# Moving the sum of the keys' rotary rotation from VectorE to GpSimd, in every step of an attention kernel

## The reference, cut to what matters

```
q = (ln(h) @ w_q)   # 16 heads of 128
k = (ln(h) @ w_k)   # 4 key heads of 128, each shared by 4 query heads
q = q * cos + rotate_half(q) * sin
k = k * cos + rotate_half(k) * sin
scores = q k^T / sqrt(128) + causal mask (window 256)
out = softmax(scores) @ v ; h = h + out @ w_o
```

## Time and profile before

| what | value |
|---|---|
| median of 3 runs | 804.98 us |
| the profiled execution | 805.23 us |
| its span, first to last instruction | 803.3 us |
| mean granted TensorE clock | 0.996 |
| PE busy | 736.1 us (92%) |
| DVE busy | 574.5 us (72%) |
| ACT busy | 445.2 us (55%) |
| POOL busy | 433.7 us (54%) |
| DMA, mean over the span | 39 GB/s |

### The profile page before, as it was taken

How to read it: one execution, slowest core, us unless ns; L and a number is a source line. 1 busy time by engine, 2 the same in 40 slices (tenths; PEclk the granted TensorE clock), 3 DMA queues, 4 the chain that set the end, 5 groups by cost and what they waited for, 6 DMA issues and landing times.

```text
span 803.3 us, 19511 instructions
## 1 busy us (share of the span) xinstructions
PE 736.1 (92%) x6910; PEld 670.9 (84%) x6910; DVE 574.5 (72%) x1602; ACT 445.2 (55%) x1237; POOL 433.7 (54%) x647
## 2 busy tenths in 40 slices
PE   0266788999999999999999999999999999999996
PEld 0156768999999999999989999999999998988883
DVE  6999967887765666766674565665666678888986
ACT  5734445665565657555574555555565656455422
POOL 1397866744434747544474564444384746565622
PEclk9999999999999999999999999999999999999999
DMA  9023751100010203000001020000020000001303
GB/s 209 13 52 77 169 151 34 47 8 8 7 47 8 67 8 96 10 7 7 7 26 41 1 93 8 7 7 3 5 68 7 29 8 8 7 7 25 87 14 91
DMA packets 38127, 31.59 MB, mean 39 GB/s; under 512 B 23790, under 2 KB 29294, under 8 KB 38070
## 3 DMA queue, kind: packets, MB, share of 16 engines
q1 hardware_dynamic: 37926, 30.78, 14.9%
q10 hardware_dynamic: 144, 0.07, 0.0%
HBM read 20.34 MB, written 10.49 MB: 38 GB/s over the span
## 4 chain that ended last, share of the span: by engine, by line
PE 83%; DVE 6%; POOL 4%; ACT 3%; issue 2%; DMA 1%; DVEq 0%; SPq 0%; POOLq 0%
PE bank_quad L1541 17%; PE bank_quad L1542 17%; PE bank_quad L1543 16%; PE bank_pair L1541 4%; PE bank_pair L1542 4%; PE bank_pair L1543 4%; PE bank_quad L1661 2%; PE bank_pair L1732 2%; PE bank_pair L1742 2%; PE bank L1742 2%; PE bank L1746 2%; PE bank L1541 2%; PE bank_quad L1553 2%; PE bank L1542 2%; PE bank L1543 1%
## 5 line engine op out<-in xcount | busy, mean ns | idle before, releaser
L1541 PE MATMUL bank_quad<-xt_hi,w_hi 128*128 128x256 f32 (+1 forms) x568 | 159.5, 281 | 0.0
L1542 PE MATMUL bank_quad<-xt_hi,w_lo 128*128 128x256 f32 (+1 forms) x568 | 158.9, 280 | 0.0
L1543 PE MATMUL bank_quad<-xt_lo,w_hi 128*128 128x256 f32 (+1 forms) x568 | 158.6, 279 | 0.0
L649 POOL TENSOR_TENSOR swap<-swap,cst 128x512 f32<-128x512 f32 (+1 forms) x96 | 105.5, 1110 | 38.4 <-ACT swap L876 38.4
L933 ACT ACTIVATE sm<-sm,mx 128x128 f32<-128x128 f32 (+1 forms) x256 | 113.6, 444 | 20.1 <-DVE mx L1407 20.1
L1238 DVE TENSOR_TENSOR kq<-kq,swap 128x512 f32<-128x512 f32 (+1 forms) x96 | 89.9, 956 | 25.9 <-POOL swap L649 24.8
L1541 PEld LDWEIGHTS bank_quad<-xt_hi,w_hi 128*128 128x128 f32 x568 | 106.8, 188 | 0.0
L1542 PEld LDWEIGHTS bank_quad<-xt_hi,w_lo 128*128 128x128 f32 x568 | 106.7, 188 | 0.0
L1543 PEld LDWEIGHTS bank_quad<-xt_lo,w_hi 128*128 128x128 f32 x568 | 106.3, 187 | 0.0
L689 POOL TENSOR_SCALAR sm<-sm,rinv 128x128 f32<-128x128 f32 (+1 forms) x256 | 103.9, 417 | 0.1
L945 ACT ACTIVATE ot_hi<-bank_quad 128x512 fp32r<-128x512 f32 x64 | 37.8, 597 | 118.4 <-PE bank_quad L1543 118.4
(11 more groups left out here) (343 smaller groups left out, 2132.3 us busy)
## 6 DMA issues: line engine op xcount, KB each, us to landing
mixed<-st SPq DMA_DIRECT2D x32, 128.0 KB
x<-mixed SPq DMA_DIRECT2D x32, 128.0 KB, 3.1
out<-x SPq DMA_DIRECT2D x32, 128.0 KB, 2.3
raw<-in_w_qkv SPq DMA_DIRECT2D x8, 384.0 KB, 3.9
raw<-in_w_o SPq DMA_DIRECT2D x10, 256.0 KB, 2.9
norm_mem<-in_w_qkv SPq DMA_DIRECT2D x6, 384.0 KB, 4.4
later_v<-v_next SPq DMA_DIRECT2D x16, 128.0 KB, 1.7
v_next<-later_v SPq DMA_DIRECT2D x16, 128.0 KB, 2.0
```

What stands on the lines that cost most here:

```text
L649: nc.gpsimd.tensor_tensor(view(sw), view(sw), table(sinT), ALU.mult).then_inc(rot_sin, 1)
L1541: mmul(dst, lh, rh, start=start and k == 0, stop=False, skip_group_check=True)
L1542: mmul(dst, ll, rh, start=False, stop=False, skip_group_check=True)
L1543: last = mmul(dst, lh, rl, start=False, stop=stop and k == n - 1, skip_group_check=True)
```

## The change

The sum of part 0, the keys, leaves DVE. POOL makes it (`keys_add`) straight behind its own product of the keys with the sines, in the prologue and in every step. It waits for `kq_cos` and `rot_sin` and signals a new semaphore, `keys_rot`. ACT waits for that one ahead of rounding the keys and ahead of the next pair's swap; the counts of `kq_rot` are now two in a pair. Three calls of `rope_add(..., 0)` go out of DVE's program.

```diff
+            def keys_add(s):
+                view, _, _, _ = rope_view(0)
+                pool.wait_ge(kq_cos, s * 3 + 1)
+                pool.wait_ge(rot_sin, s * 3 + 1)
+                nc.gpsimd.tensor_tensor(view(kq), view(kq), view(sw), ALU.add).then_inc(keys_rot, 1)
+
...
             def rotate(s):
 
-                for j in range(3):
+                rotate_sin(s, 0)
+                keys_add(s)
+                for j in (1, 2):
                     rotate_sin(s, j)
                 for j in range(3):
                     kq_rest(s, j)
...
             norm(1)
             rotate_sin(0, 0)
+            keys_add(0)
             norm(2)
...
             rotate_sin(1, 0)
+            keys_add(1)
             for n in (KC, KC + 1):
                 split_lo(n)
             normalise_probs(0)
...
-                        act.wait_ge(kq_rot, s * 3)
+                        act.wait_ge(kq_rot, s * 2)
+                        act.wait_ge(keys_rot, s)
...
-                    act.wait_ge(kq_rot, s * 3 + (j + 1))
+                    if j == 0:
+                        act.wait_ge(keys_rot, s + 1)
+                    else:
+                        act.wait_ge(kq_rot, s * 2 + j)
...
-                rope_add(i + 1, 0)
...
-            rope_add(1, 0)
```

More of the change, by code:

```diff
@@ L351, in tower @@
         minus_done, squared = sem("minus_cw_done"), sem("late_f_squared")
+        keys_rot = sem("keys_rotated")
         early_var, early_pool, early_rstd, early_xn, early_xt, early_hi, early_lo, x_early = (
@@ L1283, in _ @@
             rope(0, 1)
-            rope_add(0, 0)
             xt_rest(1)
```

## The result

After the change the kernel takes 809.05 us, the median of 7 runs (807.72 to 809.79), against 805.10 for the kernel before in 7 runs (803.83 to 806.40): a ratio of 1.0046, with a 95% interval of 1.0036 to 1.0056. It is slower by 3.95 us. The forecast was 807.6, in a range of 805.6 to 814.3. The sign and the mechanism of the prologue were right; the size was about 1.5 us short, and 809.05 lies just outside the narrower range of 806.6 to 809 that the prediction gave to the forecast itself.

A forecast was written before the change was run, and what follows sets the result against it. PE was taken to bound nearly all of the 32 steps. The terms 1.5 + 0.8 + 0.3 = 2.6 us on the median of 804.98 gave 807.6, in a range of 805.6 to 814.3 (forecast's own range 806.6 to 809).

The forecast's parts named there:

- Part 1: Prologue: keys' sum waits for VectorE's cosine product and delays GpSimd's splits and normalising, making PE late: +1.5 us (0.7 to 2.2).
- Part 2: First step: GpSimd's longer queue blocks VectorE's sums, so the low parts reach PE late: +0.8 us (0 to 1.1).
- Part 3: The 11 rotations without a values' projection: VectorE's sum wins the port by 0.12 us, nothing reaches PE: 0.
- lost race: Rival: in those 11 rotations GpSimd's last product goes first, PE waits 0.6 us each, 6.6 in all: 814.2; chance 0.20.
- Part 4: Weight split behind pair 15's rests in GpSimd's queue: PE's 0.8 us wait grows, +0.3 us (0 to 0.7).
- The steps with the gated update: There the keys' sum stands ahead of the gates' reading, which waits for PE; nothing on the way to `x` is shorter: 0.
- VectorE's relief: The 32 sums, 45.7 us, taken off VectorE were forecast to be worth nothing, as PE bounds nearly all steps.
- its own signs: Profile marks: GpSimd idle to about 128.7, normalising ending near 135.6, longer prologue wait; wrong if PE's waits after 165 change over 1 us.

The follow-up runs named there:

- experiment 2: The change with the keys' sums of pairs 0 and 1 left on DVE, so POOL sums in the steps alone: 807.32 us, ratio 1.0038 to before.
- experiment 4: The change with three more filler matmuls on PE in the wait ahead of `attend(0)`: 808.51 us, ratio 1.0052 to before.
- Experiments 5 and 6: The change with most output-weight parts cut to 128 of 512 columns, in POOL's splits (5) or ACT's roundings (6): 808.39 and 807.15 us.
- experiment 1: The change with the keys' sum on POOL in the prologue alone, back on DVE in the steps: 807.01 us, ratio 1.0025 to before.
- experiment 9: Keys' sum on POOL in the steps alone, behind all three sine products, prologue as in the kernel before: 808.10 us, ratio 1.0042 to before.
- experiment 3: The change with pair 1's keys' sum moved behind pair 0's normalising in POOL's prologue queue: 807.43 us, ratio 1.0035 to before.
- experiment 10: The kernel before with ACT's last swapped copy and DVE's cosine product for it moved earlier in the prologue: 803.42 us, ratio 0.9983.

## Why the prediction was right, and where not

**Part 1, +1.5: right in each step, but not whole.** With the 0.78 us added, the keys' sum started at 128.76 (128.75 forecast), the splits ended at 132.02 (132.05), the normalising at 135.59 (135.65), the sine product at 136.83 (136.95), the sum at 138.07 (138.2), the low parts at 139.86 (140.05), the cosine product at 140.46 (140.7). `attend(0)` was 1.47 late (1.7) and the 0.21 us wait behind it was absorbed. The wait itself is 2.96, not near 3.5, since PE came to it later, with 0.53 us for the normalised probabilities where 0.27 for the layer norm had been. The term that is missing altogether is the clock: the sum took for granted that PE goes on behind a wait of 3 us as behind one of 1.9. The drop took 1.47 us in `attend(0)`, of which 0.56 reached the end.

**Part 2, +0.8: mis-sized, and hidden in the change.** Where the clock stayed up, the stall was there at the right place but about half as large: a wait of 0.35 (experiment 2) and 0.38 (4), and +0.46 and +0.36 up to pair 1. In the change itself PE was late from the clock, and the stall found slack. Both together are the +1.00 up to pair 1, against 0.6 forecast (0.8, and the 0.21 absorbed).

**Part 3, 0: right for 9 of 11, wrong for 2.** The order was read right, and the lead was thinner than the 0.12 us said: DVE's sum came in between at 302.87, with POOL's data there since 302.84. What failed is the step from one step to eleven. The order of issue was taken from pair 8, as if POOL's third product were always released by ACT's copy. Behind ACT's roundings of the output weight POOL is 0.65 us later against that copy, and it isn't. The trace of before had shown this. There the third product waits 0.95 us for the copy in pair 8, but in pair 9 only 0.32, less than the 0.74 us that the new sum puts ahead of it:

```profile
319.58 1.73 POOL L649 TENSOR_TENSOR swap<-swap,cst 128x512 f32<-128x512 f32 x1 [0.32 <-ACT swap L876]
```

Experiments 5 and 6 tell POOL's own splits from ACT's roundings. Two steps at 0.93 are 1.9 us. Of the rival "lost race", which had 0.20, two elevenths came true.

**Part 4, +0.3: right, 0.34 in length**, 0.46 in waits, and at another row than given: the wait for `w_lo` stayed at 0.8, that for `x` ahead of it grew from 0.25 to 0.76. The path isn't the one through POOL's splits, but it starts at the delay that part 3 named. DVE's last sum of the pair starts 4.01 us ahead of pair 14's first attention product before (412.20, 416.21) and 3.47 after (415.35, 418.82). ACT rounds the keys and queries and then the next weight (`w_hi`), which starts 0.54 later in its turn; DVE takes that weight's low part and adds to `x` behind it, 0.51 later, and PE's wait grows by 0.51. In experiment 1, where DVE sums the keys in the steps, that wait didn't grow.

**The steps with the gated update, 0: right** (128.63 against 128.51); experiment 9 shows that it holds only for a sum that stands early.

**VectorE's relief** was worth nothing anywhere, as forecast. The waits of PE that are gone from the list (0.27 and 0.21 us) gave way to longer ones. Its busy time fell by 34.9 of 45.7 us, which is less than 45.7 but not "far less".

**By its own signs** the prediction held in the prologue (POOL's stall of 3.58 us, the normalising's end, the longer wait) and failed behind it. It called itself wrong if PE's waits after 165 us changed by over 1 us: they grew by 2.0, 0.77 and 0.78 for `pt_lo` and the rest at the change of group. That the result still lies in the range of 805.6 to 814.3 is due to its width, which was there for a race lost in all eleven steps.

Summed in the forecast's terms: parts 1 and 2 were 2.3 and are 1.70 with the clock up (experiment 4: 31.40 and 22.86 against 30.06 and 22.50), which with part 4's 0.3 leaves 2.0 of the 2.6. Pairs 9 and 25 add 1.86, the clock 0.56 (experiment 4 against the change) and the rest some 0.3: 4.7, as the traces show. The medians show 3.95. Two things fit the difference, and neither is shown: runs of the kernel before in which its clock fell as well, which its profiled execution doesn't have, and a profiled execution of before that was late ahead of the cut and not behind it (0.78 us against that of the change), in a part that differs by up to 2.4 us between executions of one program.

## What to carry to other kernels

An instruction that is moved into another engine's queue costs what stands behind it there while it waits for its input; put it where its input has long been there (experiment 3 took back the whole 1.47 us ahead of `attend(0)`, and 1.25 in all), and look at the clock behind any wait that this makes longer. Where two engines race for a port by a tenth of a microsecond, one step of a loop says nothing of the others: list for every kind of step what releases both, and how long each waits. Here one more row of the trace before, that of pair 9, would have told. And work taken from an engine that is seldom last was worth nothing here, while one that is last can be worth a reordering of two instructions (experiment 10).

## What the runs showed that I had not expected

- The race is all or nothing within a tenth of a microsecond. A VectorE sum of 128x512 that began at 302.87, when GpSimd's next product had its data since 302.84, ran in 0.69 us and made GpSimd stand; one that began 0.05 us behind GpSimd's second product, with the third one's data there, ran in 1.77 us. For the first of the two sums nothing in between was seen in the steps of pairs 7 to 14.
- Forcing the better order by a semaphore cost more than losing the race did in two steps: +3.4 us in all against the change by the traces (2.4 by the medians), by 0.18 us in each ordinary step, too short for a wait to show in the list, and by 2.7 at the change of group.
- Behind the same wait of 1.92 us PE's granted clock was 1.00 in three traces and fell to 0.5 in two; experiments 2 and 9, one of each kind, have the same program up to there.
